# Six product tiles per group built from triangles of points instead of one left operand per row

## The reference, cut to what matters

```python
# r_x: (2048, 39, 16), W0: (39*39, 128), W1: (39*128, 128)
x1 = einsum('bid,bjd,ijh->bhd', x, x, W0.reshape(39, 39, 128))
x2 = einsum('bid,bjd,ijh->bhd', x, x1, W1.reshape(39, 128, 128))
out = sum(concatenate([x1, x2], axis=1), axis=-1)      # (2048, 256)
```

## Time and profile before

| | us |
|---|---|
| median of 3 runs (lowest to highest) | 580.67 (578.86 to 581.48) |
| the profiled execution's own time | 579.92 |
| its span, first to last instruction | 578.1 |
| PE busy | 550.1 (95% of the span) |
| PEld / DVE / ACT / POOL busy | 483.1 / 472.1 / 470.0 / 480.9 |
| DMA packets on the hardware queue, share of 16 engines | 88.0% (163.09 MB) |

### The profile page before, as it was taken

One profiled execution on the slowest core, in us unless ns is written; L12 is line 12 of the kernel. 1 busy time (PEld: TensorE's weight loads), 2 busy tenths in 40 slices (PEclk: granted clock), 3 DMA queues, 4 the chain that ended last, 5 costly groups with the idle time before them and its releaser, 6 DMA issues.

```text
span 578.1 us, 10856 instructions
## 1 busy us (share of the span) xinstructions
PE 550.1 (95%) x3186; PEld 483.1 (84%) x3186; DVE 472.1 (82%) x816; ACT 470.0 (81%) x983; POOL 480.9 (83%) x407
## 2 busy tenths in 40 slices
PE   5788788999999999999999999999999999999998
PEld 3476677878888888988988998898889889889988
DVE  4688888888888898888889888888988888888740
ACT  4698888889888888888888888888888888888740
POOL 6998899899989888889988888898888899888800
PEclk9799999999999999999999999999999999999999
DMA  8999999999899989999999989999999989988210
GB/s 318 331 352 317 326 312 304 306 305 295 267 306 332 307 298 290 279 324 287 288 301 312 303 268 305 315 296 293 313 285 281 325 292 300 295 304 285 52 52 10
DMA packets 66489, 163.78 MB, mean 283 GB/s; under 512 B 10112, under 2 KB 18816, under 8 KB 66432
## 3 DMA queue, kind: packets, MB, share of 16 engines
q1 hardware_dynamic: 66432, 163.09, 88.0%
HBM read 139.98 MB, written 2.10 MB: 246 GB/s over the span
## 4 chain that ended last, share of the span: by engine, by line
PE 71%; ACT 10%; DMA 6%; issue 5%; POOL 4%; DVE 2%; SPq 1%; ACTq 0%; DVEq 0%; POOLq 0%
PE acc L397 12%; PE acc L399 11%; PE acc L398 11%; PE fin L448 6%; PE fin L449 6%; PE fin L450 6%; DMA outs<-w_dram 5%; PE pg L433 5%; PE pg L431 5%; PE pg L432 5%; ACT fh L510 4%; PE turn L409 4%; PE acc L392 2%; POOL fl L761 2%; ACT gh L552 1%
## 5 line engine op out<-in xcount | busy, mean ns | idle before, releaser
L761 POOL TENSOR_TENSOR fl<-fs,fh 128x512 fp32r<-128x512 f32 x192 | 249.7, 1304 | 42.8 <-ACT fh L510 40.1
L397 PE MATMUL acc<-fh,w0h 128*128 128x512 f32 x384 | 160.3, 417 | 15.3 <-ACT x L533 10.1
L756 POOL TENSOR_TENSOR fs<-xr,xs 128x512 f32<-128x512 f32 x128 | 163.0, 1295 | 0.9 <-DMA xr<-xb_dram 0.8
L647 DVE TENSOR_TENSOR fp<-xl,xr 128x512 f32<-128x512 f32 x192 | 133.5, 697 | 31.4 <-ACT xl L517 18.4
L399 PE MATMUL acc<-fl,w0h 128*128 128x512 f32 x384 | 151.9, 395 | 0.0
L398 PE MATMUL acc<-fh,w0l 128*128 128x512 f32 x384 | 151.5, 395 | 0.0
L651 DVE TENSOR_TENSOR fl<-fp,fh 128x512 fp32r<-128x512 f32 x192 | 131.9, 687 | 23.1 <-ACT fh L510 18.2
L510 ACT ACTIVATE fh<-fp 128x512 fp32r<-128x512 f32 x192 | 114.5, 596 | 36.3 <-PE acc L399 30.6
L666 DVE TENSOR_TENSOR gl<-pg,gh 128x320 fp32r<-128x320 f32 x252 | 117.0, 486 | 25.8 <-ACT gh L552 20.6
L510 ACT ACTIVATE fh<-fs 128x512 fp32r<-128x512 f32 x192 | 121.4, 632 | 10.8 <-PE acc L399 8.6
L552 ACT ACTIVATE gh<-pg 128x320 fp32r<-128x320 f32 x252 | 105.5, 439 | 18.4 <-PE pg L433 17.6
(11 more groups left out here) (67 smaller groups left out, 724.0 us busy)
## 6 DMA issues: line engine op xcount, KB each, us to landing
xr<-xb_dram SPq DMA_DIRECT2D x192, 512.0 KB, 5.7
xbd<-xdhl SPq DMA_DIRECT2D x256, 80.0 KB, 4.0
xs<-xa_dram SPq DMA_DIRECT2D x64, 256.0 KB, 4.1
xdr<-xd_dram SPq DMA_DIRECT2D x64, 160.0 KB, 3.9
xp<-xpairs_dram SPq DMA_DIRECT2D x32, 256.0 KB, 4.3
outs<-w_dram SPq DMA_DIRECT2D x9, 256.0 KB, 6.6
out_dram<-outs SPq DMA_DIRECT2D x7, 256.0 KB, 5.8
fs<-w0a_dram SPq DMA_DIRECT2D x1, 256.0 KB, 4.8
```

Source lines behind the costliest of these rows:

```text
L397: nc.tensor.matmul(acc[:, :], w0h[:, t, :], fh[:, t, :], start=t == 0, stop=False)
L647: nc.vector.tensor_tensor(f_at(t), xl[:, :], xr[:, gi % 2, t, :], ALU.mult).then_inc(prod_dve, 1)
L756: nc.gpsimd.tensor_tensor(f_at(t), xr[:, gi % 2, t, :], xs[:, gi % 2, :], ALU.mult)\
L761: nc.gpsimd.tensor_tensor(fl[:, t, :], f_at(t), fh[:, t, :], ALU.subtract).then_inc(low_pool, 1)
```

## The change

1. **Tiles from triangles.** A system of triples of the 39 points is laid out in which every pair of points lies in exactly one triple. 128 of the triples become the 128 rows. A row has an apex a and two other points b and c. Tile 0 is a*b, tile 2 is a*c, tile 1 is b*c: three products from the left operand and two right operands. The remaining pairs and squares fill tiles 3, 4 and 5 (`STARS`) with the row's apex as left operand. Tile 1 has no right operand of its own: POOL multiplies the right operands of tiles 0 and 2. So `xr` holds five right operands of 256 KB per group, in parts of two, two and one (`PARTS`): tiles 0 and 2 in part 0, tiles 3 and 4 in part 1, tile 5 in part 2. The number of tiles and of instructions on the engines stays as it was.
2. **Block input in two buffers.** `xdr` is double-buffered, and SP loads it a group further ahead (`load_xd(g+3)`), at the end of its iteration. The wait on xd_low now stands there too, behind the loads of right operands.
3. **Own buffer for second weights.** `w1r` replaces `outs` for W1 and a part of `xr` for some of W0. `w1_load` stands at the head of SP's iteration and no longer at its end. `first_out(0)` on POOL moves from group 15 to group 13.
4. In SP's iteration the first loads wait for products (g+1, 4) and (g+1, 2), before for 0 and 4. At the start, group 1's right operands no longer wait for w0_ready.

```diff
-LOADED = range(NT)
+HALF = M // 3
+PLACE = {0: 0, 2: 1, 3: 2, 4: 3, 5: 4}
+BOTH_RIGHT = 1
+NR = len(PLACE)
+PARTS = (slice(0, 2), slice(2, 4), slice(4, 5))
+PART_OF = {0: 0, BOTH_RIGHT: 0, 2: 0, 3: 1, 4: 1, 5: 2}
+STARS = (3, 4, 5)
...
+def triples():
+    def point(x, i):
+        return HALF * (i % 3) + x % HALF
+    yield from ((point(x, 0), point(x, 1), point(x, 2)) for x in range(HALF))
+    for x in range(HALF):
+        for y in range(x + 1, HALF):
+            for i in range(3):
+                yield point(x, i), point(y, i), point((x + y) * (HALF + 1) // 2, i + 1)
...
+def pair_slots(of):
+    for m, row in enumerate(of.tolist()):
+        for t, k in PLACE.items():
+            yield t, m, row[0], row[1 + k]
+        yield BOTH_RIGHT, m, row[1 + PLACE[0]], row[1 + PLACE[2]]
...
-        xr = sb("xr", [P, 2, NT, GC])
+        xr = sb("xr", [P, 2, NR, GC])
...
-        xdr = sb("xdr", [P, 2, NQ, MI])
+        xdr = sb("xdr", [P, 2, 2, NQ, MI])
...
+        w1r = sb("w1r", [P, NW, H])
...
             def w1_load(p):
                 if p:
                     sp.wait_ge(w1_ready, p)
                     sp.wait_ge(w1_ready_dve, p)
+                else:
+                    sp.wait_ge(w0_ready, 3)
                 sp.dma_start(w1_raw(p), w1[:, piece(p), :]).then_inc(w1_in, 16)
...
+                    if (first or second) and 0 <= g + 1 - W1_SLOT < PIECES:
+                        w1_load(g + 1 - W1_SLOT)
                     if more3:
-                        wait_product(sp, g + 1, 0)
                         wait_product(sp, g + 1, 4)
+                        wait_product(sp, g + 1, 2)
                         load_x(j, gi + 3)
                         load_right(j, gi + 3, 0)
                     blocks(g, gi, first)
...
-                    if not (last and gi + 1 >= CB):
-                        sp.wait_ge(xd_low, g + 2)
-                    if more2:
-                        load_xd(g + 2)
                     if more3:
                         wait_product(sp, g + 1, 3)
                         load_right(j, gi + 3, 1)
                     if more3:
                         wait_product(sp, g + 1, 5)
                         load_right(j, gi + 3, 2)
-                    if (first or second) and 0 <= g + 1 - W1_SLOT < PIECES:
-                        w1_load(g + 1 - W1_SLOT)
+                    if not (last and gi + 1 >= CB):
+                        sp.wait_ge(xd_low, g + 2)
+                    if more3:
+                        load_xd(g + 3)
...
             load_right(0, 1, 0)
+            load_right(0, 1, 1)
+            load_right(0, 1, 2)
             load_xd(0)
-            load_right(0, 1, 1)
             sp.dma_start(idn[:, :], ident).then_inc(ident_in, 16)
-            sp.wait_ge(w0_ready, 3)
-            load_right(0, 1, 2)
-            wait_product(sp, 0, 0)
+            load_xd(1)
             wait_product(sp, 0, 4)
+            wait_product(sp, 0, 2)
...
             def product(j, gi, t, fresh):
                 g = CB * j + gi
-                if t == POOL_PROD[0]:
+                if t == BOTH_RIGHT:
+                    left, place = xr[:, gi % 2, PLACE[0], :], PLACE[2]
+                else:
                     pool.wait_ge(xs_in[gi % 2], 16 * nth(j, gi))
-                pool.wait_ge(xr_in[t // 2][gi % 2], 16 * nth(j, gi))
+                    left, place = xs[:, gi % 2, :], PLACE[t]
+                pool.wait_ge(xr_in[PART_OF[t]][gi % 2], 16 * nth(j, gi))
                 if not fresh:
                     wait_low(pool, g - 1, t)
-                nc.gpsimd.tensor_tensor(f_at(t), xr[:, gi % 2, t, :], xs[:, gi % 2, :], ALU.mult)\
-                  .then_inc(prod_pool, 1)
+                nc.gpsimd.tensor_tensor(f_at(t), xr[:, gi % 2, place, :], left, ALU.mult).then_inc(prod_pool, 1)
...
-                if c == 0:
-                    pool.wait_ge(w1_ready, PIECES)
-                    pool.wait_ge(w1_ready_dve, PIECES)
...
-                    if gi == (CB - 1 if second else 5) and not first:
+                    if gi == 5 and not first:
                         first_out(j - 1, not odd)
```

More of the change, by code:

```diff
@@ L44 @@
 HIGH = (0, 1, 2, 4, 3, 5)
-NU = NT // 2
+NU = len(PARTS)
 W0_PART = 4
@@ L70, in pieces_before, with labels @@
     return min(-(-row // NW), PIECES)
[L73 to L79, removed]
+def triples():
[6 more added lines that the diff above has]
+                yield point(x, i), point(y, i), point((x + y) * (HALF + 1) // 2, i + 1)
+def labels():
+    system = list(triples())
+    whole = {k * len(system) // P for k in range(P)}
+    count = [0] * M
+    rows = []
+    for triple in (system[k] for k in sorted(whole)):
+        apex = min(triple, key=lambda v: (count[v], v))
+        count[apex] += 1
+        rows.append((apex, *(v for v in triple if v != apex)))
+    pairs = [(t[k], t[l]) for n, t in enumerate(system) if n not in whole
+             for k, l in ((0, 1), (0, 2), (1, 2))]
+    pairs += [(i, i) for i in range(M) if i not in LEFT]
+    cap = [len(STARS) * c for c in count]
+    held = {v: [] for v in range(M)}
     def settle(pair, tried):
@@ L98, in pair_slots @@
         assert settle(pair, set())
-    free = {v: [(t, m) for t in LOADED for m in range(v, P, M)] for v in cap}
-    return [(*free[v].pop(), v, i + j - v) for v, got in held.items() for i, j in sorted(got)]
+    out = []
+    for apex, b, c in rows:
+        out.append((apex, b, c, *(sum(held[apex].pop()) - apex for _ in STARS)))
+    return np.array(out)
+def pair_slots(of):
[3 more added lines that the diff above has]
+        yield BOTH_RIGHT, m, row[1 + PLACE[0]], row[1 + PLACE[2]]
 def left_rows(u):
@@ L170, in build @@
         sq_ready = sem("sq_ready")
-        xd_in = sem("xd_in")
+        xd_in = [sem("xd_in0"), sem("xd_in1")]
         xd_high = sem("xd_high")
@@ L201, in w1_raw @@
         def w1_raw(p):
-            rows = outs[:, :, :].rearrange("p a b -> p (a b)").rearrange("p (n h) -> p n h", h=H)
-            return rows[:, 0:piece(p).stop - piece(p).start, :]
+            return w1r[:, 0:piece(p).stop - piece(p).start, :]
         def tile_n(g, t):
@@ L278, in load_xd @@
             def load_xd(g):
-                sp.dma_start(xdr[:, :, :, :], xd[g]).then_inc(xd_in, 16)
+                sp.dma_start(xdr[:, g % 2, :, :, :], xd[g]).then_inc(xd_in[g % 2], 16)
             def w0a_load(k):
@@ L370, in _ @@
             load_right(0, 2, 2)
+            sp.wait_ge(xd_low, 1)
+            load_xd(2)
             chunk(0, True, False, False)
@@ L536, in xd_split @@
                 g = CB * j + gi
-                act.wait_ge(xd_in, 16 * (g + 1))
+                act.wait_ge(xd_in[gi % 2], 16 * nth(j, gi))
                 if not fresh:
                     act.wait_ge(xbd_in[gi % 2], 16 * (BQ // 2) * (nth(j, gi) - 1))
-                nc.scalar.activation(xdhl[:, gi % 2, :, :, 0, :], xdr[:, :, :, :], COPY).then_inc(xd_high, 1)
+                nc.scalar.activation(xdhl[:, gi % 2, :, :, 0, :], xdr[:, gi % 2, :, :, :], COPY).then_inc(xd_high, 1)
             def turned_high(g):
@@ L764, in xd_split @@
                 pool.wait_ge(xd_high, g + 1)
-                nc.gpsimd.tensor_tensor(xdhl[:, gi % 2, :, :, 1, :], xdr[:, :, :, :],
+                nc.gpsimd.tensor_tensor(xdhl[:, gi % 2, :, :, 1, :], xdr[:, gi % 2, :, :, :],
                                         xdhl[:, gi % 2, :, :, 0, :], ALU.subtract).then_inc(xd_low, 1)
@@ L827 @@
     xt = x.transpose(1, 0, 2).reshape(M, NG, GC)
-    xa = np.ascontiguousarray(xt[np.arange(P) % M].transpose(1, 0, 2))
+    of = labels()
+    xa = np.ascontiguousarray(xt[of[:, 0]].transpose(1, 0, 2))
     rows = [*PICKED, *LEFT]
@@ L840 @@
     xd = xd.reshape(NG, P, 2, NQ, MI)
-    right = np.zeros((FULL, P), np.int64)
     w0a = np.zeros((P, len(ORDER), H), w0.dtype)
     w0b = np.zeros((P, len(ORDER), H), w0.dtype)
-    for t, m, i, j in pair_slots():
+    for t, m, i, j in pair_slots(of):
         w0a[m, ORDER.index(t)] = w0[i, j]
@@ L848 @@
             w0b[m, ORDER.index(t)] = w0[j, i]
-        right[t, m] = j
     for u in range(2):
@@ L852 @@
             (w0b if what == "weight's low" else w0a)[m, ORDER.index(FULL) + u] = w0[i, i]
-    xb = np.ascontiguousarray(xt[right[list(LOADED)]].transpose(2, 1, 0, 3))
+    xb = np.ascontiguousarray(xt[of[:, 1:].T].transpose(2, 1, 0, 3))
     arrays = {
```

10 lines of the change are left out of this document (4 added, 6 removed).

## The result

The changed kernel is slower: 600.2 us (median of 4 runs, 598.68 to 602.39) against 580.03 us (4 runs, 578.86 to 581.48), a ratio of 1.0349 [1.0308, 1.0391], where the brackets hold the 95% interval. I had predicted 574.7 us and a range of 570.5 to 580.0 us. The profiled execution took 600.40 us, 20.48 us more than that of before.

The account below looks back on a forecast made before the run. PE was taken to bound the steady stage, with ACT's waits for W1 loads delaying PE earlier. Terms 5.3 + 0.9 - 0.2 = 6.0 us took the median of 580.67 us to 574.7 us; range 570.5 to 580.0 us.

Parts of the forecast that it names:

- What the load at the head holds back: Groups 6 to 14: xs, part 0 and blocks go out later, still 1.4 us before PE needs them; cost 0.
- Blocks late (slower): Groups 6 to 14: PE waits for late block landings, up to 1.6 us per group, 589 us in all; chance 0.12.
- The W1 stage: W1 load at the head ends ACT's waits for W1 pieces: 1.8 + 3.5 = 5.3 us saved, bounds 0 and 6.4.
- The triangles and the new steady waits: Steady stage: 256 KB fewer loads per group worth 0, hidden by PE; SP's wait for product 2 costs 0.
- The start: First groups: double-buffered xdr ends ACT's waits, saving 0.9 us; later xd(0) costs 0.2 us.
- My rival on the clock: TensorE's clock fall at 21 to 27 us: absent saves 3 us (chance 0.07), longer costs as much (0.05).

Follow-up runs that it names:

- e1: Changed kernel with the W1 load back at the end of SP's iteration, its own buffer kept; 576.92 us, ratio 0.9945.
- e3: Changed kernel with the W1 load directly behind the block DMAs; 577.01 us, ratio 0.9941.
- e4: Changed kernel, load still at the head, with three xdhl buffers, W1 through outs, first_out in group 15, right part 2 waiting for W0; 578.42 us.
- e5: Changed kernel, load still at the head, W1 pieces alternating between w1r and outs, first_out in group 15; 577.34 us, ratio 0.9932.
- e7: e3 with right part 2 of group 1 waiting for W0 again; 576.3 us, ratio 0.9932.
- e6: Kernel before the change with only the W1 load moved directly behind the block DMAs; 578.08 us, ratio 0.9965.
- e10: Kernel before the change with the triangles alone: new tiles, five right operands, first loads waiting on products 4 and 2; 578.1 us, ratio 0.9967.
- e8: e3 with DVE's low part of the squares moved behind low part 3; 575.37 us, ratio 0.9913.
- e11: e8 repeated unchanged, in more rounds; 575.37 us, ratio 0.9919.
- e12: e3 with DVE's low part of the squares moved later in chunk 0 only; 574.58 us, ratio 0.9901.

## Why the prediction was wrong

**The step that failed** is the term "What the load at the head holds back", which I took as 0. Its first half was right: SP waits for POOL's low part, and the blocks go out after it. I forecast 109.3 - 106.2 = 3.1 us from the end of the wait to the issue of the last block; in the loop above it is 109.47 - 106.32 = 3.15 us. For its landing I took 4.2 us; there it was 5.13 us. (The clock times cannot be compared: mine were iteration 10 on before's clock, and in after the last block of iteration 10 goes out at 120.2 us.) The fault is in whom I asked. I looked for the reader of what the blocks deliver, PE at 114.89 us, and found 1.4 us to spare. The blocks also hold their source: ACT's high part of the block input of group g+2 goes into the `xdhl` buffer that blocks(g) read. In before, that instruction runs at 111.89 us, 3.0 us ahead of PE. Against it, my own 113.5 us were 1.6 us late, at the median landing. The diff does not touch that wait, but it stands in `xd_split` of the kernel, between two lines that it does change.

This is not a matter of one late transfer, since ACT's high part is also the first step of what SP waits for. So each group starts later by what the last one lost, and the period becomes the loop's own, 10.7 us. Shown: e1 and e3 (the load elsewhere), e4 (the reuse taken away, the blocks as late in their iteration as ever) and e5 (the wait satisfied) each cut the loop in another place, and each ends ACT's waits on block DMAs and brings the stage from 114.75 to between 93.10 and 95.80 us. The theory that triangles, DMA order or clock made the stage long is out: e5 keeps the first two of these. For the clock there is the chain from 82 to 158 us, which has no step of PE. The changed kernel's falls of the clock in the stage, 17 us at 0.50 in all, are absent from e3 and e5, whose PE is busy 69.75 of the 70 us from 100 to 170, so they came with the pauses and did not make the loop.

**The rival "Blocks late (slower)"** had the queue, the groups and nearly the price: 1.6 us per group, where ACT's waits are 16.5 / 9 = 1.8 us. It had the wrong waiter, and so the chance (0.12) that belongs to a wait which comes only with the longest landings. Its own mechanism was real but small: in e4, where the larger wait is gone, PE stands idle for 3.2 us in three groups as the blocks land. That its price came near is luck. The profiled time would have been 573.9 + 14.4 = 588.3 us by this rival and was 600.40 us. Of the 12.1 us between them 7.9 lie in this stage (17.0 longer, where the rival has 14.4 - 5.3 = 9.1) and 4.3 in the start (3.6 longer, where it has 0.7 shorter).

**The W1 stage.** The gain was there, but not behind this placement: 5.3 us predicted, and 97.78 - 93.1 = 4.7 us measured in e3, e5 and e7. It needs one cure only. e6 (the load moved), e10 (256 KB fewer per group) and e3 (both) all take 93.10 to 93.28 us. The cures do not add up, since from there on PE sets the time: in e3 it is busy 69.75 of the 70 us from 100 to 170.

**The triangles and the new steady waits** were rightly put at 0: 368.81 of 370 us for PE, the DMA share down from 0.93 to 0.87 (I had said by a tenth), and 394.59 us from group 16 to 63, before 394.68. The waits on product 2 cost nothing.

**The start** was predicted 0.7 us shorter (0.9 - 0.2) and came out 3.6 us longer in the profiled execution, of which, by the executions with the same start, some 1.4 us belong to the change and the rest is scatter. The parts that I named did happen. ACT waits 0.29 us for xd(0) where I took 0.2 us. Its waits for `xdr` at 20.93 and 28.06 us are gone, and the copy of group 1 comes at 29.68 us, 0.8 us earlier than before's 30.48. What I did not see comes behind it. DVE's timeline in the changed kernel:

```profile
33.01 0.70 DVE L685 TENSOR_TENSOR fp<-xl,xr 128x512 f32<-128x512 f32 x1
33.74 2.66 DVE L693 TENSOR_TENSOR sq<-xp,sq 64x512 fp32r<-64x512 f32 x1
...
38.44 0.68 DVE L699 TENSOR_TENSOR x1tl<-turn,x1th 128x512 fp32r<-128x512 f32 x1
```

POOL's timeline, and PE's, of the same kernel at that time:

```profile
33.32 2.54 POOL L801 TENSOR_TENSOR fl<-fs,fh 128x512 fp32r<-128x512 f32 x2
36.07 1.07 POOL L805 TENSOR_TENSOR xdhl<-xdr,xdhl 128x320 fp32r<-128x320 f32 x1 [0.21 <-ACT xdhl L578]
```

```profile
39.18 0.63 PE L469 MATMUL pg<-xbd,x1th 128*128 128x320 f32 x1 [2.21 <-DVE x1tl L699]
```

The squares' low part took 2.66 us beside POOL's two low parts, DVE's `x1tl` came about 2 us later for it, and PE paused 2.21 us, from 36.97 to 39.18 us. Within this pause, at 38.5 us, the granted clock fell to 0.50, and stayed there for 6.8 us. In e8, with that instruction moved, DVE and PE show:

```profile
34.98 0.69 DVE L693 TENSOR_TENSOR sq<-xp,sq 64x512 fp32r<-64x512 f32 x1
```

```profile
37.04 0.41 PE L469 MATMUL pg<-xbd,x1th 128*128 128x320 f32 x1 [0.82 <-DVE x1tl L699]
```

The pause is 0.82 us, and the clock stays at 1.00 from 38.5 to 41.5 us, where e3's mean is 0.53. e8, e11 and e12 all have group 5 at 60.98 to 61.36 us, against 63.99 in e3. That this move avoids the second fall is shown by three profiled executions without it, against four with the same loads and the old place (after, e1, e3, e5) that all have it; how much of after's start it cost is argued from the traces.

My rival on the clock spoke of the first fall only, and priced it at 3 us. In after this fall was half as long as before's (3.4 against 6.8 us) and group 1's copy came only 0.8 us earlier. In e8 it lasted 6.8 us again, in e3 3.4 us, and the copies of group 1 are at 28.84 and 28.98 us: the first fall is hidden, the second is not.

## What to carry to other kernels

A transfer has two customers: the one that reads what it delivers, and the one that will overwrite what it reads. When a wait moves a transfer back, look up both in the code, and ask whether the earlier one is itself a step of what the wait waits for; if so, what looks like one late microsecond is a loop, and its length is the new period. A wait that is moved to the head of an in-order queue costs what the most impatient thing behind it costs; place it behind those, or make it one that is already satisfied. And several cures of one wait are worth one of them: once PE is full, the second gives nothing. Last, a wait that a profile ascribes to nobody is still a wait: in e4 the landing times of the DMAs named it.

## What the runs showed of the hardware

**A DVE instruction beside POOL.** The same DVE subtraction of 64x512 from SBUF took 0.69 us in e8, where it began as POOL's run of low parts ended, and 2.66 us in the changed kernel beside POOL's back-to-back low parts, and it ended at 36.40 us, 0.5 us after these (33.32 + 2.54 = 35.86 us). DVE's products, of which one operand lies in PSUM, took 0.68 to 0.70 us beside the same POOL work. The Trainium skill ("SBUF — State Buffer", Who interferes with whom) says that a DVE instruction with two SBUF inputs and a GpSimd instruction that reads SBUF contend, that this is an exclusive lock and issue order decides who blocks, while a DVE instruction with at most one SBUF input (outside the two-port modes) does not contend. The trace agrees, in 2.66 against 0.69 us. It is a price of the place in the order, not of the instruction: it was 690 ns in the steady stage at the old place and 1031 ns at the new.

**The clock.** In the changed kernel the granted clock fell to 0.50 (1.2 GHz) at 38.5 us, within a pause of PE of 2.21 us, and in e8 with a pause of 0.82 us there it did not. The length of a single pause does not tell it: in e11 the clock fell at 87.3 us for 3.4 us, and PE had paused only 0.83 us before 85.71 and 0.29 us before 87.17 us. That W1 stage is 1.4 us longer than e8's.

**W1 landings.** The same 256 KB landed in 2.7 us at the median in the changed kernel, with SP's queue just emptied, in 5.0 us in e10 and in 6.7 us in before. By this comparison less than half of before's time was the transfer's own.
